# A fused cross-attention and feed-forward kernel: group 0's norm and turn in the last attention steps, and the feed-forward groups interleaved with the front of what follows

## The reference

```
x = x + latent_cross_attention(ctx, layernorm(x), mask)      # A: 2 heads
x = x + two_layers(layernorm(x))                             # B and F, two layers
x = x + cross_attention(layernorm(x), ctx)                   # C: 8 heads
x = x + quantised_gated_ffn(layernorm(x))                    # D

def layer(x):                                                # one layer of B and F
    q, k, v = split(shift_token(x) @ wqkv)                   # 8 heads of 64
    q, k = rotary(l2norm(q) * qs, l2norm(k) * ks)
    x = x + local_attention(q, k, v) @ wo                    # windows of 64, one back
    h = layernorm(shift_token(x)) * lg + lb                  # F begins here
    a, g = split(h @ w1 + b1)                                # 341 columns each
    return x + (a * gelu(g)) @ w2 + b2
```

## Time and profile before

| | |
|---|---|
| median of the runs | 760.63 us |
| profiled execution | 757.68 us |
| its span | 755.9 us |
| TensorE busy | 636.0 us (84%) |
| VectorE busy | 567.4 us (75%) |
| ScalarE busy | 489.0 us (65%) |
| GpSimd busy | 385.7 us (51%) |
| granted TensorE clock, mean | 0.943 |

### The profile page before, as it was taken

One profiled execution on the slowest core, in us unless ns is written; L12 is line 12 of the kernel. 1 busy time (PEld: TensorE's weight loads), 2 busy tenths in 40 slices (PEclk: granted clock), 3 DMA queues, 4 the chain that ended last, 5 costly groups with the idle time before them and its releaser, 6 DMA issues. The chain is left out here.

```text
span 755.9 us, 15909 instructions
## 1 busy us (share of the span) xinstructions
PE 636.0 (84%) x5547; PEld 437.0 (58%) x5547; DVE 567.4 (75%) x1451; ACT 489.0 (65%) x1423; POOL 385.7 (51%) x425
## 2 busy tenths in 40 slices
PE   2799997889999869868999997799699999998543
PEld 1366654556766655635666766456477777776312
DVE  4767786879999746458999996464577777777486
ACT  1577864878999733238899988232577777775343
POOL 5857859998999401079999993110111222212300
PEclk9999999999999989989999999899899999998765
DMA  8600000010111110011111111000000000000001
GB/s 240 142 1 1 2 1 8 22 24 22 37 22 23 23 61 1 0 40 22 26 33 23 23 23 23 1 0 1 0 2 2 1 2 2 1 2 1 1 0 56
DMA packets 20218, 17.26 MB, mean 23 GB/s; under 512 B 7234, under 2 KB 15884, under 8 KB 20044
## 3 DMA queue, kind: packets, MB, share of 16 engines
q1 hardware_dynamic: 19308, 16.25, 8.7%
q10 hardware_dynamic: 832, 0.00, 0.1%
HBM read 8.91 MB, written 1.05 MB: 13 GB/s over the span
## 5 line engine op out<-in xcount | busy, mean ns | idle before, releaser
L1146 ACT ACTIVATE pc<-PS,nb,rsq 128x128 f32<-128x128 f32 x256 | 114.0, 463 | 2.7 <-DVE nb L1497 2.1
L753 PE MATMUL PS<-wqkv,hB 128*128 128x512 f32 x192 | 105.7, 635 | 4.7 <-DVE rsin L1483 1.8
L1204 ACT ACTIVATE pc<-PS,nb 128x256 f32<-128x256 f32 x128 | 59.0, 473 | 45.0 <-DVE nb L1647 45.0
L761 PEld LDWEIGHTS PS<-ident,rot 128*128 128x128 f32 x256 | 32.3, 146 | 55.9 <-issue 35.9
L447 POOL TENSOR_TENSOR rsk<-btmp,neghalf 128x8 f32<-128x8 f32 x32 | 60.5, 1890 | 5.9 <-POOL btmp L442 5.9
L1647 DVE TENSOR_REDUCE nb<-PS 128x2 f32<-128x512 f32 x64 | 40.8, 679 | 25.2 <-PE PS L935 25.2
L447 POOL TENSOR_TENSOR rsq<-btmp,neghalf 128x8 f32<-128x8 f32 x32 | 53.6, 1674 | 5.9 <-POOL btmp L442 5.9
L761 PE MATMUL PS<-ident,rot 128*128 128x128 f32 x256 | 40.6, 283 | 18.9 <-POOL rot L557 17.4
L1506 DVE TENSOR_TENSOR pc<-pc,rden 128x512 f32<-128x512 f32 x64 | 53.1, 830 | 2.2
L551 POOL TENSOR_TENSOR rot<-rot,rsin 128x512 f32<-128x512 f32 x32 | 40.9, 1277 | 25.8 <-DVE rsin L1483 25.8
L1146 ACT ACTIVATION_READ_ACCUMULATOR pc<-PS,nb,rsq 128x1 f32 x256 | 53.6, 209 | 0.0
(11 more groups left out here) (232 smaller groups left out, 1717.0 us busy)
## 6 DMA issues: line engine op xcount, KB each, us to landing
V<-V SPq DMA_DIRECT2D x48, 128.0 KB, 2.2
wqkv<-in_L_ffn_wqkv SPq DMA_DIRECT2D x2, 768.0 KB, 5.0
out<-x SPq DMA_DIRECT2D x4, 256.0 KB, 2.3
x<-in_x SPq DMA_DIRECT2D x1, 768.0 KB, 6.6
ctxT<-in_ctxT SPq DMA_DIRECT2D x1, 768.0 KB, 6.9
w<-in_L_ffn_w SPq DMA_DIRECT2D x2, 341.0 KB
ctxs<-in_ctx SPq DMA_DIRECT2D x1, 576.0 KB, 7.8
gel<-in_bands SPq DMA_DIRECT2D x1, 512.0 KB, 8.2
```

Source lines behind the costliest of these rows:

```text
L753: i = mm(ps, hB[:, b % 2, j * P:(j + 1) * P], wqkv[:, w * INNER:(w + 1) * INNER], start=True, stop=True)
L761: i = tr(ps[:, c * P:(c + 1) * P], rot[:, t % 2 * 2 + (name == "qT"), c * P:(c + 1) * P], ident[:])
L1146: i = af(pc[:, g % 2, par, c * P:(c + 1) * P], c_bank(g, par)[:, c * P:(c + 1) * P], ACT.Exp, bias=nb[:, g % 2, at], scale=rsq[:, g % 8, 2 ...
L1204: i = af(pc[:, u % 2, par, n * S:(n + 1) * S], c_bank(u, par)[:, n * S:(n + 1) * S], ACT.Exp, bias=nb[:, u % 2, par * 2 + n:par * 2 + n + ...
```

## The change

F is no longer a program of its own. Group 0's shift moves to step 11 of the attention, its statistics and norm to step 12, its turn to step 13 and its three up pairs to steps 14, 15 and 16; group 1's shift and turn to steps 13 and 15, group 2's shift to step 15. Groups 1 to 3 run as up, down-projection of the group before, up, turn, shift, up. Between these stand, in layer 0, the pieces of layer 1's tiles 0 to 4 and two of its scores (F_FRONT, F_LAST), and in layer 1, the k, v and token pieces of C's first sequence (F_SECOND). The turned tokens h2T get two buffers. The feed-forward's matmuls use the two pairs of banks of the scores (f_bank) instead of three pairs, and its other pieces go round the three banks with the rest (f_piece). ScalarE loads the gelu table in step 14 and the exponential's after the last gelu. The loads on SP are split and wait for less.

```diff
+F_TAIL = {T - 5: [("s", 0)], T - 3: [("s", 1)], T - 1: [("u", 1), ("s", 2)]}
+F_FRONT = {1: ([("t", 0)], [("t", 1), ("k", 0), ("q", 0)]),
+           2: ([("t", 2), ("k", 1)], [("kT", 0), ("v", 0), ("qT", 0), ("q", 1)]),
+           3: ([("t", 3), ("k", 2), ("kT", 1)], [("v", 1), ("qT", 1), ("q", 2)])}
+F_LAST = ([("t", 4), ("k", 3), ("kT", 2)], [("v", 2), ("qT", 2), ("q", 3)])
+F_SECOND = {1: (["k01"], ["k23"]), 2: (["v0"], ["v1"]), 3: (["t"], [])}
-C_FIRST = ["k01", "k23", "v0", "v1", "t", "q01", "q23"]
+C_FIRST = ["q01", "q23"]
-        h2T = sb("h2T", [P, 512])
+        h2T = sb("h2T", [P, 2, 512])
+        def f_bank(G, c, k):
+            return PS[:, (G % 4 * 3 + c) % 2 * 2 + k, :]
...
+            shifted_values(0, range(T))
+            projections(1)
             _, k, turn = b_piece("W", T - 1)
             sp.wait_ge(bank_full[k], turn + 1)
-            attention_weights(1)
+            output_weights(1)
+            shifted_values(1, range(2))
             sp.wait_ge(sem("y_ready"), B + B + FIRST)
             ffn_weights(1)
-            shifted_values(1)
+            shifted_values(1, range(2, T))
...
+            def f_up(G, c):
+                layer, n = G // 4, G % 4 * 3 + c
+                if c == 0:
+                    _, k, turn = f_piece("u", G)
+                    pe.wait_ge(bank_free[k], 2 * turn + 2)
+                if n == 0:
+                    pe.wait_ge(sem("ld_w12"), layer * (12 * 16) + 12 * 16)
+                if n < 2:
+                    for par in range(2):
+                        pe.wait_ge(pT_full[par], A_UNITS + layer * T + T - 1 + n)
+                else:
+                    pe.wait_ge(sem("F_hh"), layer * 12 + n - 1)
+                c0, m = HCH[c]
+                mm(f_bank(G, c, 1)[0:m, :], w1[:, HID + c0:HID + c0 + m], h2T[:, G % 2], start=True, stop=True).then_inc(sem("F_gate"), 1)
+                mm(f_bank(G, c, 0)[0:m, :], w1[:, c0:c0 + m], h2T[:, G % 2], start=True, stop=True).then_inc(sem("F_up"), 1)
...
+            def f_groups(layer):
+                for g in range(1, 4):
+                    G = layer * 4 + g
+                    f_up(G, 0)
+                    f_make("d", G - 1)
+                    f_up(G, 1)
+                    if g < 3:
+                        f_make("u", G + 1)
+                    if g < 2:
+                        f_make("s", G + 2)
+                    for part in range(2):
+                        for name, at in f_front(layer, F_FRONT[g][part]):
+                            b_make(name, 1, at % T)
+                        if layer:
+                            pe.wait_ge(sem("ld_C"), 6 * 16)
+                            for name in F_SECOND[g][part]:
+                                c_make(name, 0)
+                        if part == 0:
+                            f_up(G, 2)
+                            if g == 3 and layer == 0:
+                                pe.wait_ge(sem("F_hh"), 11)
+                                b_scores(1, 0)
+                f_make("d", layer * 4 + 3)
...
+            def f_groups(layer):
+                for g in range(1, 4):
+                    G = layer * 4 + g
+                    f_gate(G, 0)
+                    if g < 3:
+                        f_apply(G + 1)
+                    f_residual(G - 1)
+                    f_gate(G, 1)
+                    if g < 2:
+                        f_shifted(G + 2)
+                    if layer and g == 2:
+                        c_sum(0)
+                    if layer and g == 3:
+                        c_norm(0)
...
+                    f_gate(G, 2)
...
+                f_residual(layer * 4 + 3)
```

More of the change, by code:

```diff
@@ L386, in ffn_weights, with shifted_values @@
                 load(b2[:], t_in["L0_ffn_b2"][layer:layer + 1, :].broadcast_to([P, D]), "ld_w12")
-            attention_weights(0)
+            projections(0)
+            output_weights(0)
+            gains(0)
             ffn_weights(0)
             later_loads()
-            def shifted_values(layer):
-                for t in range(T):
+            def shifted_values(layer, tiles):
+                for t in tiles:
                     _, k, turn = b_piece("v", layer * T + t)
@@ L824, in b_step @@
                     b_make(name, layer, g % T)
+                if step == T - 3:
+                    f_make("u", layer * 4)
                 if 0 <= step + 2 < T:
@@ L1167, in b_step @@
                         b_copy(g, par)
+                if step == T - 3:
+                    f_copy(layer * 4)
                 pieces("k", "t")
@@ new lines, in b_step, with f_copy, f_gelu @@
+                for name, G in f_tail(layer, step):
+                    if name == "u":
+                        f_copy(G)
+            def f_copy(G):
+                ps, k, turn = f_piece("u", G)
+                if G % 4 == 0:
+                    act.wait_ge(sem("ld_w12"), G // 4 * (12 * 16) + 12 * 16)
+                act.wait_ge(bank_full[k], turn + 1)
+                af(h2T[:, G % 2], ps, ACT.Identity, scale=lnB[:, 0:1], bias=lnB[:, 1:2]).then_inc(bank_free[k], 2)
+            def f_gelu(G, c):
+                c0, m = HCH[c]
+                act.wait_ge(sem("F_gate"), G * 3 + c + 1)
+                af(gel[0:m, c, :], f_bank(G, c, 1)[0:m, :], ACT.Gelu, bias=b1[0:m, 1, c:c + 1]).then_inc(sem("F_gel"), 1)
@@ L1227, in c_take @@
                 i.then_inc(bank_free[k], 2)
+            for u in FIRST_STEPS:
+                a_step(u)
+                if u - A_UNITS in B_STEPS:
+                    b_step(0, u - A_UNITS)
+            f_groups(0)
+            b_take("t", 1, 4)
+            b_exps(T, 1)
+            b_take("k", 1, 3)
+            b_exps(T, 0)
+            b_take("kT", 1, 2)
+            for name, at in f_front(0, F_LAST[1]):
+                b_take(name, 1, at % T)
+            for step in range(T + 1):
+                b_step(1, step)
+            f_groups(1)
             for name in C_FIRST:
@@ L1524, in b_step @@
                     b_scale(g + 1, 1)
+                if step == T - 4:
+                    f_shifted(layer * 4)
                 if 0 <= step + B_AHEAD["k"] < T:
```

388 lines of the change are left out of this document (206 added, 182 removed).

## The result

The changed kernel takes 723.74 us (median of 4 runs, 722.43 to 724.43); the kernel before took 760.25 in the runs beside it. The ratio is 0.9516, with an interval of 0.9495 to 0.9538. The forecast was 723.6. The profiled execution took 724.43, its span is 722.6 instead of 755.9, and its mean granted clock 0.958 instead of 0.943.

A forecast was written before the change was run, and what follows sets the result against it. Between attention's end and the next part's first output, TensorE waits at reduced clock. Savings of 28.0 and 10.7 less 1.7 give 37.0: span 718.9, execution 720.7, with the median 3.0 above, 723.6 us; range 713 to 738.

The forecast's parts named there:

- the seams: Stretches from step 12's output copy to the next part's first, after layers 0 and 1: 28.0 and 10.7 us less.
- Tail, 3.0 us late: Last attention steps, both layers: added feed-forward pieces, notably GpSimd's half copy before step 12's maximum, delay the last output 3.0 us.
- Rival C: Tail: each feed-forward piece in VectorE's order delays the loop, 6.4 us more per layer, 736 us; chance 0.13.
- B: Rival: tail hides its additions (6.0 us over both layers), start-up stays at full clock (3 us); 715 us; chance 0.15.
- Groups of layer 0, 43.5: Layer 0's feed-forward groups 1 to 3 and last down-projection, with layer 1's pieces between, take 43.5 us on TensorE.
- Rival D: Layer 0's groups: rotations waiting for GpSimd pace the fill, 52.5 us for 35.7, 17 more in seam 1, 740; chance 0.09.
- E: Rival: with two pairs of banks instead of three, up pairs in the groups wait for gates; 785 us; chance 0.03.
- Fill, 7.4: From layer 0's last group to layer 1's first output: GpSimd's work on the fourth k stretches 4.95 us to 7.4.
- Groups of layer 1, 34.0: Layer 1's groups with cross-attention pieces take 34.0 us, including bare waits on the norm (1.6) and last gate (1.0).
- Start-up, 14.6: Cross-attention, from q01 to first output copy: a chain of maximum, exponentials and turns that stays at 14.6 us.
- A: The main case, all terms as worked out: 723.6 us, own range 717 to 730; chance 0.60.
- Table loads at nothing: ScalarE's gelu load in step 14 lies beside TensorE's work, exp's behind the last gelu; cost nothing, uncovered 1.28 us each.

The follow-up runs named there:

- e4: Changed kernel with only the second part's first norm moved, on VectorE, ahead of the residual and second gate of layer 1's last group; 721.48 us.
- e10: Changed kernel with half copy, second part's norm and fill's last k earlier, plus tile 2's turned-k copy and last q's rotation earlier; 718.46 us.
- e11: e10 with one change more in layer 1's fill: VectorE rotates the last tile's q ahead of both maxima, not between them; 724.20 us.

## Why the prediction was right, and where not

- **The forecast of 723.6** was met (723.74), partly by luck: I had worked out a span of 718.9, and it was 722.6. The 3.0 us that I added because the median of before lay that far above its profiled execution hid most of the miss; after, the median lies 0.7 below the profiled execution. The span's 3.7 are 3.5 that the seams gave less than I had said and 1.9 at the start, less the allowance of 1.7.
- **Body unchanged:** right, 8.58 us a step. The 1.7 us allowance for small waits has nothing to show for it.
- **Tail, 3.0 us late:** 2.64 (25.60 for 22.96), with the half copy as named: VectorE waited 2.00 for it for the earlier trace rows's copy, and the maximum came 2.3 late. Group 1 began 24.2 us after the old place of step 12's output, for 24.7 predicted. My check "last output copy 18.3 after step 12's" reads 15.7, since step 12's copy moved too; the claim should have been put from step 11. Rival C (over 23) is out, and so is B: it had the tail hide its additions.
- **Groups of layer 0, 43.5:** 43.6 (10.9, 12.0, 13.1 and 7.6 for 10.9, 11.8, 13.0 and 7.8). Rival D's 60.3 is out. TensorE never waited for a gate by a microsecond in them, so two pairs of banks do and E is out.
- **Fill, 7.4: the step that failed.** It took 11.5, and the 4.1 are the whole difference between 28.0 and 24.3 in seam 1, less the 0.4 gained in the tail. I had priced one chain, the fourth k up to GpSimd's product. The values start at 333.85 as that chain allows (7.2 after the group's end at 326.63; the earlier trace rows is answered by the chain's row at 326.65), but the output copy stands in VectorE's order behind the next tile's k, two maxima and a scaling, and starts at 338.13. That order was in the code; I stopped at TensorE. The change did not make this lag: before, the copy of 360.28 came 3.84 after its values, now 4.28. My sum, which was to end at the copy, left it out. Of the three orders tried, one gained 0.3, one nothing more, and one lost 4. TensorE and VectorE in order of time, before and now:

```profile
356.44 1.15 PE L804 MATMUL PS<-pT,V 128*64 128x64 f32 x32
```

```profile
333.85 1.15 PE L860 MATMUL PS<-pT,V 128*64 128x64 f32 x32
...
335.11 0.67 DVE L1601 TENSOR_REDUCE mx<-PS 128x4 f32<-128x512 f32 x1
...
336.72 0.69 DVE L1614 TENSOR_TENSOR pc<-pc,rden 128x512 f32<-128x512 f32 x1
337.33 0.68 DVE L1601 TENSOR_REDUCE mx<-PS 128x4 f32<-128x512 f32 x1
```

- **Groups of layer 1, 34.0:** 34.3, with the two bare waits as named: 1.52 on the norm (1.6) and 1.00 on the last gate (1.0). e4 shows that the first was free to take away.
- **Start-up, 14.6:** 14.53, still at half clock for more than half of it (granted clock 0.71, before 0.79), as A had it and B had not. TensorE in order of time:

```profile
492.60 0.41 PE L964 MATMUL PS<-ident,hn 128*128 128x128 f32 x2 [1.52 <-DVE hn L1763]
...
495.72 2.92 PE L882 MATMUL PS<-w,rot 128*128 128x128 f32 x24 [1.00 <-DVE rot L1704]
498.48 1.89 PE L975 MATMUL PS<-hT,wqC 128*128 128x256 f32 x8
...
504.62 1.95 PE L1004 MATMUL PS<-ident,pc 128*128 128x128 f32 x8 [0.71 <-DVE pc L1798]
508.98 2.08 PE L994 MATMUL PS<-big 64*128 64x256 f32 x8 [2.41 <-ACT pT L1304]
```

- **Table loads at nothing:** right. Gelu's load of step 14 ends at 272.57 and the gelu starts at 272.90, when its matmul is done: nothing is drained in between, as in the earlier trace rows. The drain of 1.38 us that the Trainium skill adds (ScalarE: Activation LUTs, "What ACT_TABLE_LOAD costs") did not show; nor did the 1.3 us that I had estimated from it for the end of each tail (0.9 by my own cover of 1.8), since group 1 began 24.2 us after that mark for 24.7 without it. Exp's load behind the last gelu cost nothing either: ScalarE stood idle after it in both layers, 1.46 us in layer 0 and 3.71 in layer 1.

```profile
271.29 1.28 ACT L1253 ACT_TABLE_LOAD   x1
272.90 0.69 ACT L1271 ACTIVATE gel<-PS,b 128x512 f32<-128x512 f32 x1 [0.33 <-PE PS L900]
```

What stays open: why the clock fell in four of 16 tails and not in the others with the same waits, and how far the fill would shrink if its order on VectorE were laid out anew.

## What to carry to other kernels

Where one program runs out and the next fills up, lay matmuls of the one into the waits of the other: here the gain was the waits and, on top, the clock that they had cost. Work it out as a sum over the busiest engine's new queue, then follow the last result to the instruction that reports it, on its own engine and in that engine's order; the one term that I stopped short on was the one that was wrong. And measure from a mark that the change can't move.

## What the runs showed of the hardware

A VectorE instruction with both inputs in SBUF does not end before a GpSimd sum or product over 512 columns that was under way when it started. `nb`, a product of four numbers a partition, takes 0.16 us alone; it took 0.93 beside GpSimd's product in e10 and 0.78 beside its sum in the changed kernel (at 335.82). Nor is this rare: in the changed kernel 23 of the 64 `nb` started inside such a sum, took 0.52 to 1.00, and each ended 0.02 us after it. Over all 14 traces it is 340, and one alone ended before GpSimd's instruction, the one in e11 at 337.75 that started in the same moment. A scaling of 128 by 512, 0.69 us alone, ended at least 0.55 after the sum or product beside which it started and took up to 1.74 (356 cases). The rotation's two passes, which read PSUM, never took more than 0.69 beside the same instructions (478 cases). So far it agrees with the Trainium skill, "SBUF — State Buffer", section "SBUF: two separate sides": VectorE and GpSimd share one pair of ports, held for a whole instruction by whichever starts first, and a VectorE operation with two SBUF inputs needs it. By that sentence GpSimd's power over 8 columns, which reads SBUF too, should block as well. It does not: beside it (`rsk`, at 324.97 in e11) a scaling kept its 0.69, and all 391 `nb` that started beside a power kept 0.16 to 0.17. The effect runs the other way too: GpSimd's small instruction ahead of the power (`btmp`, 8 columns) takes 0.24 us, and 0.68 in the 25 of 64 cases of the changed kernel in which one of VectorE's scalings was running when it started (one other case took as long). The profile shows the effect as a longer instruction, not as a wait. I had not reckoned with it in the fill.
